# Order of the first blocks: a quarter of a projection and x's first transposes moved, exponentials in front of a unit's passes

## The chip, the cores and the metric

The kernel runs on one core of a Trainium2 chip. Its engines are TensorE (PE; its weight loads are shown apart as PEld), VectorE (DVE), ScalarE (ACT), GpSimd (POOL) and SyncE (SP), which here only issues transfers. Every engine works through its own list of instructions in the order in which they were written; semaphores hold an instruction until what it needs is there. The metric is the device time of one execution in microseconds (us), the median of several.

## The reference

Six sub-layers of a decoder work on x, 8 sequences of 128 rows of 512 numbers, all in float32. Only the first is touched by the change; the second and the fifth matter because their preparations lie in the same stretch.

```python
x = layernorm(x + L0_attn(x))            # 8 heads of width 8, softmax over 128 keys
x = layernorm(x + L0_xattn(ctx, ctx, x)) # softmax(ctx x^T / sqrt(128)) over the keys
x = layernorm(x + L0_ffn(x))             # a routed low-rank addition
x = layernorm(x + L1_attn(x))            # weights looked up from 16-level codes
x = layernorm(x + L1_xattn(x, ctx))      # scores through Wq^T Wk
x = layernorm(x + L1_ffn(x))

def L0_attn(x):
    qk = (x @ Wqk.T + bqk).reshape(b, n, 8, 8, 2)
    v = (x @ Wv.T + bv).reshape(b, n, 8, 8)
    attn = softmax(q @ k^T) / 8
    return (attn @ v) @ Wo.T + bo
```

L1_attn's weights are `NF4[codes] * scales`: an integer code of 0 to 15 picks one of 16 numbers, and a scale per 64 columns multiplies it.

## The kernel before

The 1024 rows of x are cut into 8 tiles of 128, one to a sequence. The first attention is a loop over these tiles, called blocks here, t = 0 to 7. PE's part of block t is, in order: `max_rows(t)` (turns the row maxima of the scores), `o_proj(t-1)` (the output projection of the tile before), `scores_T(t)` (the scores again, transposed and with the maximum subtracted), `x_T(0, t-2)` (the normed x of two tiles before, transposed for the second sub-layer), `scores(t+1)`, and `heads_out(t)` (probabilities times values). Between them stand pieces of work that belong to later sub-layers and fill PE's time: `key_step(n)`, n = 0 to 15, four products each of which sum up to one quarter of Wq^T Wk in PSUM bank 0, and `key_biases`. In blocks 3, 4 and 5 four key steps run: one behind `max_rows`, one behind `scores_T`, and two behind `heads_out`. The first of these last two starts a new quarter in bank 0 and so waits on `kw_ready`, until ACT has copied the quarter before out of the bank. In block 6 `key_biases(4)` waits in the same way at the end.

ACT's part of block t from t = 2 on is `unit_bends(t-1, 0)`, `heads_exp(t)` (the exponentials of `scores_T(t)`), `x_T_out(t-2)` (copies the transposes to SBUF), `key_group_out` (the copy of a finished quarter that `kw_ready` stands for), `unit_bends(t-1, 1)` and `norm_tail(t-1)` (the last step of the layer norm). A bend is one pass over 128x1024 codes with a piecewise linear function; six passes and two joins on DVE look up one chunk of L1_attn's weights. `unit_bends(u, part)` is one or two passes: for odd u one pass in each part, for even u two. So part 0 of block t has one pass at t = 2, 4, 6 and two at t = 3, 5, 7.

`scores(t+1)` waits until `heads_exp(t)` has read the scores' banks; `max_rows` waits for DVE's row maximum of the new scores; `x_T(0, t-2)` waits for `norm_tail(t-2)`. ACT's passes over the second chunk of codes wait for its transfer. DVE's share is the row maximum, the addition of the maximum to the queries, the division by the sums, the layer norm's statistics and the joins.

The order is written out by hand. Behind the loop come `sims(0)`, `o_proj(7)`, `x_T(0, 6)`, which waits for `norm_tail(6)`, and `keys(0)`, the first of the long products of the second sub-layer's stage.

Of the kernel before, what the change touches and what calls it, by code (L numbers as in the profile page):

```python
# [18 lines left out]
NT = 8  # L19
T = NT * P  # L20
D = 512
KD = D // P
# [87 lines left out]
def key_span(t):  # L110

    first = 2 + KD * (t - 3)
    return (max(0, first), min(first + KD, KD * KD))
# [22 lines left out]
def decoder_kernel(nc, i, out):  # L136
# [4 lines left out]
    with ctx:  # L141
# [3 lines left out]
        def sem(name):  # L145
            return ctx.enter_context(nc.semaphore(name))
# [252 lines left out]
        qk_ps, qk_ready, place_ps, q_placed, k_placed, v_ps, vT_ready, vt_ps, v_ready = (sem(n) for n in ("qk_ps", "qk_ready", "place_ps", "q_placed", "k_placed", "v_ps", "vT_ready", "vt_ps", "v_ready"))  # L399
# [202 lines left out]
        def _(pe):  # L602
# [10 lines left out]
                for n in range(times):  # L613
                    pe.matmul(bank[1][:, 0:HG * P], mz[:, 0, :], mz_flat, start=True, stop=True)

            def qk_projection(n):

                if n == 0:
                    pe.wait_ge(in_qk, 16)
                pe.wait_ge(in_x[n], 16)  # L620
                if n >= 2:
                    pe.wait_ge(qk_ready, (0, 0, 1, 3)[n])
                for h in range(2) if n == 0 else (0,):
                    size = P if n == 0 else PC
                    if h:
                        pe.wait_ge(in_x0b, 16)
                    t = slice(n * PC + h * P, n * PC + h * P + size)
                    for k in range(KD):
                        last = pe.matmul(bank[QK_BANK[n]][:, h * P:h * P + size], qkT[:, k, :], xT[:, k, t], start=(k == 0), stop=(k == KD - 1))
                last.then_inc(qk_ps, 1)  # L630

            def values(m):

# [12 lines left out]
            def v_rows(m):  # L646

                pe.wait_ge(vT_ready, m + 1)
                if m:
                    pe.wait_ge(ln_sum, m)  # L650
                for b in range(4):
                    h = b // 2
                    part = slice(h * HA, (h + 1) * HA)
                    dst = bank[V_BANK[h]][:, PC + b % 2 * HA:PC + (b % 2 + 1) * HA]
                    last = pe.transpose(dst, vT[part, m * PC + b % 2 * P:m * PC + (b % 2 + 1) * P], ident[part, part])
                last.then_inc(vt_ps, 1)
# [10 lines left out]
            def scores(b):  # L667
                if b >= 2:
                    pe.wait_ge(in_heads[b // 2], 16 * HI)
                else:  # L670
                    pe.wait_ge(q_placed, 1)
                    pe.wait_ge(k_placed, 1)
                if b >= 1:
                    pe.wait_ge(p_ready, b)
                t = slice(b * P, (b + 1) * P)
                for g in range(HG):
                    for n in range(HI):
                        rows = slice(n * ROWG, n * ROWG + HK)
                        last = pe.matmul(head_scores[:, n, g, :], qT[rows, g, t], kT[rows, g, t], start=True, stop=True)
                last.then_inc(s_ps, 1)  # L680

            def max_rows(b):

                pe.wait_ge(max_ready, b + 1)
                for g in range(HG):
                    last = pe.transpose(max_T[:, g, :], mz[:, g, :], ident[:, :])
                last.then_inc(max_ps, 1)

            def scores_T(b):
                pe.wait_ge(aug_ready, b + 1)  # L690
                t = slice(b * P, (b + 1) * P)
                for g in range(HG):
                    for n in range(HI):
                        rows = slice(n * ROWG, n * ROWG + HK)
                        last = pe.matmul(head_scores[:, n, g, :], kT[rows, g, t], q_aug[rows, b % 2, g, :], start=True, stop=True)
                last.then_inc(sT_ps, 1)

            def heads_out(b):

                pe.wait_ge(p_ready, b + 1)  # L700
                pe.wait_ge(v_ready, b // 4 + 1)
                if b >= 1:
                    pe.wait_ge(att_ready, b)
                for cols, lhs in ((slice(0, P), lambda g, n: vx[:, b, g, n, :]), (slice(P, 2 * P), lambda g, n: ones8[:, g, :])):
                    for g in range(HG):
                        for n in range(HI):
                            last = pe.matmul(bank[1][n * ROWG:(n + 1) * ROWG, cols], lhs(g, n), pT[:, b % 2, n, g, :],
                                             start=(g == 0), stop=(g == HG - 1))
                last.then_inc(pv_ps, 1)

            def o_proj(b):
                pe.wait_ge(att_ready, b + 1)
                if b == 0:
                    pe.wait_ge(in_xn, 48)
                else:
                    pe.wait_ge(ln_sum, b)
                    pe.wait_ge(v_ready, 2)
                pe.matmul(bank[7][:, :], attT[:, b % 2, :], wo0[:, :], start=True, stop=True).then_inc(o_ps, 1)
# [13 lines left out]
            def key_step(n):  # L732

                c, d = divmod(n, KD)
                if n == 0:
                    pe.wait_ge(qk_ready, NP)
                    pe.wait_ge(in_wk, 16 * KD)
                    pe.wait_ge(in_wq, 16)
                elif d == 0:
                    pe.wait_ge(kw_ready, c)  # L740
                last = pe.matmul(bank[0][:, :], wk1[d][:, c * P:(c + 1) * P], wq1[:, d, :], start=(d == 0), stop=(d == KD - 1))  # L741
                if d == KD - 1:
                    last.then_inc(kw_ps, 1)
# [68 lines left out]

            warm_up(WARM)
            qk_projection(0)
            warm_up(2)
            place_heads()
# [2 lines left out]
            values(0)  # L819
            pe.wait_ge(ident_ready, 1)  # L820
            max_rows(0)
            v_rows(0)
            scores_T(0)
            qk_projection(2)
            scores(1)
            heads_out(0)
            values(1)
            for t in range(1, NT):
                steps = range(*key_span(t)) if t > 1 else range(0)
                max_rows(t)  # L830
                for n in steps[0:1] if 2 < t < NT - 1 else ():
                    key_step(n)
                if t == 2:
                    v_rows(1)
                    key_step(0)
                o_proj(t - 1)
                scores_T(t)
                if t == 1:
                    qk_projection(3)
                elif t == NT - 1:  # L840
                    key_biases(KD + 1)
                for n in steps[1:2]:
                    key_step(n)
                if t > 1:
                    x_T(0, t - 2)
                if t + 1 < NT:
                    scores(t + 1)
                heads_out(t)
                for n in steps[2:]:
                    key_step(n)  # L850
                if t == NT - 2:
                    key_biases(KD)
# [329 lines left out]
            def t_products(j, b):  # L1182

                w = t_dn_part(j)
                return down_products(t_d_bank(b)[:, :], b, (hidden_part(xh, j), hidden_part(xl, j)), (w, w), j == 0, j == T_END[-1])
# [23 lines left out]
            for b in range(NT):  # L1209
                for j in T_END:  # L1210
                    if b == 0:
                        t_landed(j)
                    last = t_products(j, b)
# [4 lines left out]
        def _(act):  # L1218
# [43 lines left out]
            def unit_bends(u, part):  # L1262

                early_bends(2 * u + part + LEAD)
# [19 lines left out]
            def key_group_out(c):  # L1284
                act.wait_ge(kw_ps, c + 1)
                if c < KD:
                    nc.scalar.activation(kq_w[:, c, :], bank[0][:, :], ACT.Copy).then_inc(kw_ready, 1)
                else:
                    nc.scalar.activation(folded[:, c - KD, :], bank[0][:, :], ACT.Copy).then_inc(kw_ready, 1)
# [26 lines left out]
            def heads_exp(b):  # L1316
                act.wait_ge(sT_ps, b + 1)
                if b >= 2:
                    act.wait_ge(pv_ps, b - 1)
                nc.scalar.activation(pT[:, b % 2, :, :, :].rearrange("p i g t -> p i (g t)"),  # L1320
                                     head_scores.rearrange("p i g t -> p i (g t)"), ACT.Exp).then_inc(p_ready, 1)
# [26 lines left out]
            for t in range(2, NT):  # L1348
                if t == NT - 1:
                    key_group_out(KD)  # L1350
                unit_bends(t - 1, 0)
                heads_exp(t)
                x_T_out(t - 2)
                if t > 2:
                    key_group_out(t - 3 if t < NT - 1 else KD + 1)
                unit_bends(t - 1, 1)
                norm_tail(t - 1)
# [976 lines left out]
```

## Time and profile before

| | us |
|---|---|
| median of 3 runs | 644.88 (644.25 to 645.72) |
| the profiled execution's own time | 645.23 |
| its span in the trace | 643.1 |
| PE busy | 632.0 |
| DVE busy | 396.3 |
| ACT busy | 381.6 |

The granted clock of PE over the execution was 0.998 of full speed. The blocks 1 to 7 lie between 21 and 70 us of the span, `x_T(0, 6)` at 72.6. Busy time is the time in which an engine has an instruction under way. A start and a duration are given for each group of instructions; consecutive instructions of one engine overlap by some 0.1 us, so that what one costs its engine in a row is the distance from its start to the next start. PE is busy for nearly all of the span; the time in brackets behind a row is how long its engine had been idle.

### The profile page before, as it was taken

Reading aid. Unit: us, or ns where it says so; the run is one execution under the profiler, and the core shown is the slowest. Engines: PE = TensorE matmul, PEld = TensorE weight load, DVE = VectorE, ACT = ScalarE, POOL = GpSimd, SP = SyncE. Lnnn points to the kernel's source line nnn. Section 1 sums busy time; section 2 is a strip of 40 time slices with the busy share of each in tenths; the row PEclk is TensorE's granted clock in tenths of the full one; section 3 lists DMA queues with packets and bytes.
Section 4 is the critical chain, followed back from the end, with each engine's and each line's share of the span. In section 5 each row is a group of like instructions: output and inputs, shape, how many; then the busy total and the mean of one; then the engine's idle time right before and its main releaser. Section 6 shows DMA issues by size and latency. Waiting matters only on the chain.

```text
span 643.1 us, 8521 instructions
## 1 busy us (share of the span) xinstructions
PE 632.0 (98%) x3226; PEld 470.0 (73%) x3226; DVE 396.3 (62%) x633; ACT 381.6 (59%) x527; POOL 65.0 (10%) x116
## 2 busy tenths in 40 slices
PE   9999999999999999999999999999999999999996
PEld 6655555544558888888888888887777888888874
DVE  4798787667988777767667355335655212125467
ACT  2977789976987697576675154223565343316532
POOL 1032142311330000000000000001211000000012
PEclk9999999999999999999999999999999999999999
DMA  7771585512253134233320003056010322100002
GB/s 246 288 243 52 188 268 172 162 52 92 81 152 120 39 110 139 73 104 111 94 83 2 1 1 131 1 216 274 1 33 2 115 77 88 33 1 0 1 33 99
DMA packets 25590, 63.92 MB, mean 99 GB/s; under 512 B 5541, under 2 KB 10725, under 8 KB 24782
## 3 DMA queue, kind: packets, MB, share of 16 engines
q1 hardware_dynamic: 23294, 61.68, 29.4%
q10 hardware_dynamic: 2256, 1.70, 0.8%
q8 instruction: 26, 0.43, 0.3%
q14 instruction: 14, 0.11, 0.1%
HBM read 58.77 MB, written 4.60 MB: 99 GB/s over the span
## 4 chain that ended last, share of the span: by engine, by line
PE 88%; DVE 4%; ACT 4%; DMA 1%; issue 1%; SPq 1%; POOL 0%; POOLq 0%; DVEq 0%; ACTq 0%
PE bank L1043 18%; PE bank L1031 8%; PE bank L1030 8%; PE bank L1032 8%; PE bank L1122 8%; PE bank L1121 8%; PE bank L882 4%; PE bank L802 3%; PE bank L606 3%; PE bank L741 2%; PE bank L1097 1%; DMA codes<-in_c_qkv 1%; PE bank L912 1%; PE bank L926 1%; PE bank L984 1%
## 5 line engine op out<-in xcount | busy, mean ns | idle before, releaser
L1232 ACT ACTIVATE line<-line 128x1024 f32<-128x1024 f32 x87 | 91.4, 1050 | 0.2
L1030 PE MATMUL bank<-xh,wh 128*128 128x512 f32 x224 | 87.5, 391 | 0.0
L1031 PE MATMUL bank<-xl,wh 128*128 128x512 f32 x224 | 87.5, 391 | 0.0
L1032 PE MATMUL bank<-xh,wl 128*128 128x512 f32 x224 | 87.3, 390 | 0.0
L1043 PE MATMUL bank<-wh,xh 128*128 128x512 f32 x192 | 76.1, 396 | 0.2 <-DVE xl L2128 0.2
L1043 PE MATMUL bank<-wh,xl 128*128 128x512 f32 x192 | 74.9, 390 | 0.0
L2211 DVE SCALAR_TENSOR_TENSOR arena<-bank,ff_s,arena 128x512 f32<-128x512 f32 x28 | 21.0, 752 | 72.9 <-PE bank L1122 63.8
L2128 DVE TENSOR_TENSOR xl<-arena,xh 128x1024 fp32r<-128x1024 f32 (+1 forms) x26 | 29.7, 1141 | 35.4 <-ACT xh L1536 35.3
L1121 PE MATMUL bank<-xh,wh 128*128 128x512 f32 x128 | 50.3, 393 | 0.0
L1536 ACT ACTIVATE xh<-arena 128x1024 fp32r<-128x1024 f32 (+1 forms) x26 | 25.6, 991 | 41.3 <-PE bank L1043 34.8
L1122 PE MATMUL bank<-xl,wh 128*128 128x512 f32 x128 | 49.9, 390 | 0.0
L1032 PEld LDWEIGHTS bank<-xh,wl 128*128 128x128 f32 x224 | 42.1, 188 | 8.8
L1030 PEld LDWEIGHTS bank<-xh,wh 128*128 128x128 f32 x224 | 42.1, 188 | 8.5
L1031 PEld LDWEIGHTS bank<-xl,wh 128*128 128x128 f32 x224 | 42.1, 188 | 8.5
L1630 ACT ACTIVATE arena<-bank,ff_s 128x512 f32<-128x512 f32 x28 | 19.2, 686 | 43.4 <-PE bank L1122 43.4
L1512 ACT ACTIVATE arena<-bank 128x512 f32<-128x512 f32 x28 | 16.4, 586 | 46.9 <-PE bank L1032 46.9
L1695 POOL TENSOR_TENSOR rstd<-rstd,minus_half 128x1 f32<-128x1 f32 x40 | 26.7, 668 | 172.1 <-DVE rstd L2149 162.4
L1043 PEld LDWEIGHTS bank<-wh,xh 128*128 128x128 f32 x192 | 36.1, 188 | 8.3 <-DVE xl L2128 0.6
L1043 PEld LDWEIGHTS bank<-wh,xl 128*128 128x128 f32 x192 | 36.1, 188 | 7.5
L1121 PE MATMUL bank<-xh,wl 128*128 128x512 f32 x96 | 37.6, 391 | 0.0
L1745 DVE SCALAR_TENSOR_TENSOR line<-line 128x1024 f32<-128x1024 f32 x29 | 35.3, 1218 | 3.6 <-ACT line L1232 3.2
L1043 PE MATMUL bank<-wl,xh 128*128 128x512 f32 x96 | 37.4, 390 | 0.0
(219 smaller groups left out, 1264.3 us busy)
## 6 DMA issues: line engine op xcount, KB each, us to landing
codes<-in_c_gu SPq DMA_DIRECT2D x14, 512.0 KB, 3.8
scales<-in_s_gu SPq DMA_DIRECT2D x28, 256.0 KB, 4.0
codes<-in_t_gu SPq DMA_DIRECT2D x8, 512.0 KB, 4.2
codes<-in_c_dn SPq DMA_DIRECT2D x7, 512.0 KB, 4.6
scales<-in_s_dn SPq DMA_DIRECT2D x14, 256.0 KB, 3.9
fold<-in_t_dn SPq DMA_DIRECT2D x1, 3584.0 KB, 15.7
codes<-in_c_qkv SPq DMA_DIRECT2D x6, 512.0 KB, 4.8
scales<-in_t_gu SPq DMA_DIRECT2D x6, 512.0 KB, 3.8
```

The source lines that it names most:

```text
L882: pe.matmul(bank[FF_BANK[b % 3]][:, :], xT[:, k, b * P:(b + 1) * P], w0T[:, k, :], start=(k == 0), stop=False)
L1030: pe.matmul(dst, wh[:, s, c:c + P], xh[:, k, cols], start=(k == 0), stop=False)
L1031: pe.matmul(dst, wh[:, s, c:c + P], xl[:, k, cols], start=False, stop=False)
L1032: last = pe.matmul(dst, wl[:, s, c:c + P], xh[:, k, cols], start=False, stop=(k == KD - 1))
L1043: ins = pe.matmul(dst, h[:, b * P:(b + 1) * P], w, start=first and p == 0, stop=last and p == len(hiddens) - 1)
L1121: pe.matmul(dst, w[:, c:c + P], xh[:, k, cols], start=(k == 0), stop=False)
L1122: last = pe.matmul(dst, w[:, c:c + P], xl[:, k, cols], start=False, stop=(k == KD - 1))
L1232: nc.scalar.activation(below(slot), below(slot), ACT.Prelu, bias=bias, scale=scale, alpha=alpha).then_inc(bent, 1)
L1536: nc.scalar.activation(dst[:, cols], hT[:, j, cols], ACT.Copy).then_inc(done, 1)
L1695: last = nc.gpsimd.tensor_tensor(rstd[:, m % 2, 1:2], rstd[:, m % 2, 0:1], minus_half[:, :], ALU.pow)
L1745: nc.vector.scalar_tensor_tensor(weight(slot), weight(slot), -NEAR_UP, below(slot), ALU.max, ALU.subtract).then_inc(joined, 1)
L2128: nc.vector.tensor_tensor(low[:, cols], hT[:, j, cols], f32(hi[:, cols]), ALU.subtract).then_inc(done, 1)
```

## The change

Three things move; nothing is added or taken away.

- A quarter of a projection. `qk_projection(2)` is a sum over four parts of the 512 columns, each one product of 128x128 by 128x256. Its first part is now issued behind `max_rows(0)` and in front of `v_rows(0)`; the other three stay behind `scores_T(0)`. Both pieces add into bank 0.
- x's first transposes. `x_T(0, 0)` in block 2 stood in front of `scores(3)` and now stands behind `heads_out(2)`. The lines on `key_step` are written in another way, with the same order.
- Exponentials. In the blocks 2 to 7 ACT now does `heads_exp(t)` first and `unit_bends(t-1, 0)` behind it.

```diff
-            def qk_projection(n):
+            def qk_projection(n, steps=range(KD)):
...
-                    for k in range(KD):
+                    for k in steps:
                         last = pe.matmul(bank[QK_BANK[n]][:, h * P:h * P + size], qkT[:, k, :], xT[:, k, t], start=(k == 0), stop=(k == KD - 1))
-                last.then_inc(qk_ps, 1)
+                if KD - 1 in steps:
+                    last.then_inc(qk_ps, 1)
...
             max_rows(0)
+            qk_projection(2, range(1))
             v_rows(0)
             scores_T(0)
-            qk_projection(2)
+            qk_projection(2, range(1, KD))
...
                 max_rows(t)
-                for n in steps[0:1] if 2 < t < NT - 1 else ():
-                    key_step(n)
                 if t == 2:
                     v_rows(1)
-                    key_step(0)
+                for n in steps[0:1] if t < NT - 1 else ():
+                    key_step(n)
                 o_proj(t - 1)
...
-                if t > 1:
+                if t > 2:
                     x_T(0, t - 2)
                 if t + 1 < NT:
                     scores(t + 1)
                 heads_out(t)
+                if t == 2:
+                    x_T(0, 0)
                 for n in steps[2:]:
                     key_step(n)
...
             for t in range(2, NT):
                 if t == NT - 1:
                     key_group_out(KD)
+                heads_exp(t)
                 unit_bends(t - 1, 0)
-                heads_exp(t)
                 x_T_out(t - 2)
```

PE's list in block 2 before, from `scores_T(2)` on: L695 is `scores_T`, L741 a key step, L606 `x_T`, L679 `scores`, L707 `heads_out`, L686 `max_rows`.

```order
50 L695 MATMUL bank<-fold,heads 128x128 [waits aug_ready]
51 L695 MATMUL bank<-fold,heads 128x128 x7
52 L741 MATMUL bank<-arena 128x512
53 L606 MATMUL bank<-ident,x 128x128 [waits v_ready,ln_done]
54 L606 MATMUL bank<-ident,x 128x128 x3
55 L679 MATMUL bank<-heads 128x128 [waits p_ready,in_heads1]
56 L679 MATMUL bank<-heads 128x128 x7
57 L707 MATMUL bank<-fold,project 32x128 [waits att_ready,v_ready,p_ready]
58 L707 MATMUL bank<-fold,project 32x128 x7
59 L707 MATMUL bank<-fold 32x128 x8
```

The same place in the changed kernel, where every line number above 625 is one higher:

```order
53 L742 MATMUL bank<-arena 128x512
54 L680 MATMUL bank<-heads 128x128 [waits p_ready,in_heads1]
55 L680 MATMUL bank<-heads 128x128 x7
56 L708 MATMUL bank<-fold,project 32x128 [waits att_ready,v_ready,p_ready]
57 L708 MATMUL bank<-fold,project 32x128 x7
58 L708 MATMUL bank<-fold 32x128 x8
59 L606 MATMUL bank<-ident,x 128x128 [waits v_ready,ln_done]
60 L606 MATMUL bank<-ident,x 128x128 x3
61 L687 MATMUL bank<-ident,fold 128x128 [waits max_ready]
```

The four transposes have moved from in front of the scores to between `heads_out(2)` and `max_rows(3)`.

ACT's list in block 3 before: L1224, L1226, L1232 and L1240 are passes over codes, L1320 the exponentials, L1274 `x_T_out`, L1287 `key_group_out`, L1281 `norm_tail`.

```order
31 L1224 ACTIVATE line<-codes 128x1024 [waits joined,in_codes0]
32 L1226 ACTIVATE line<-codes 128x1024
33 L1320 ACTIVATE fold<-bank 128x1024 [waits pv_ps,sT_ps]
34 L1274 ACTIVATE arena<-bank 128x4x128 [waits xt_ps]
35 L1287 ACTIVATE fold<-bank 128x512 [waits kw_ps]
36 L1232 ACTIVATE line<-line 128x1024 [waits bent]
```

And in the changed kernel, where these numbers are three higher:

```order
31 L1323 ACTIVATE fold<-bank 128x1024 [waits pv_ps,sT_ps]
32 L1227 ACTIVATE line<-codes 128x1024 [waits joined,in_codes0]
33 L1229 ACTIVATE line<-codes 128x1024
34 L1277 ACTIVATE arena<-bank 128x4x128 [waits xt_ps]
35 L1290 ACTIVATE fold<-bank 128x512 [waits kw_ps]
36 L1235 ACTIVATE line<-line 128x1024 [waits bent]
```

The two passes now stand between the exponentials and the two copies out of PSUM. Blocks 5 and 7 read alike; in blocks 2, 4 and 6 it is one pass.

## Rows read from the trace of the kernel before

**Rows 1.** The page: busy us, share of the span, instructions.

```profile
PE 632.0 (98%) x3226; PEld 470.0 (73%) x3226; DVE 396.3 (62%) x633; ACT 381.6 (59%) x527; POOL 65.0 (10%) x116
```

**Rows 2.** The chain of waits in order of time: start us, us, what.

```profile
19.06 7.09 DMA codes<-in_c_qkv
...
71.84 0.71 ACT x L1281
```

**Rows 3.** Timeline of PE, block 0: start us, us, instructions [idle before, released by].

```profile
15.05 0.34 PE L655 MATMUL bank<-ident,project 64*128 64x64 f32 x4 [0.27 <-ACT project L1308]
15.32 0.73 PE L695 MATMUL bank<-fold,heads 9*128 9x128 f32 x16
15.98 1.99 PE L629 MATMUL bank<-arena,early_w 128*128 128x256 f32 x8
17.91 0.73 PE L679 MATMUL bank<-heads 9*128 9x128 f32 x16
```

**Rows 4.** Timeline of PE, blocks 2 and 3.

```profile
30.17 0.73 PE L695 MATMUL bank<-fold,heads 9*128 9x128 f32 x16
30.82 1.13 PE L741 MATMUL bank<-arena 128*128 128x512 f32 x2
31.79 0.60 PE L606 MATMUL bank<-ident,x 128*128 128x128 f32 x4
32.77 0.73 PE L679 MATMUL bank<-heads 9*128 9x128 f32 x16 [0.38 <-ACT fold L1320]
...
34.84 0.44 PE L686 MATMUL bank<-ident,fold 128*128 128x128 f32 x2 [0.33 <-DVE fold L1852]
...
40.89 1.98 PE L741 MATMUL bank<-arena 128*128 128x512 f32 x4
```

**Rows 5.** Timeline of ACT, blocks 2 and 3.

```profile
30.68 1.04 ACT L1232 ACTIVATE line<-line 128x1024 f32<-128x1024 f32 x1
31.62 1.00 ACT L1320 ACTIVATE fold<-bank 128x1024 f32<-128x1024 f32 x1
...
37.87 1.02 ACT L1320 ACTIVATE fold<-bank 128x1024 f32<-128x1024 f32 x1 [0.90 <-PE bank L695]
39.33 0.60 ACT L1274 ACTIVATE arena<-bank 128x512 f32<-128x512 f32 x1 [0.44 <-PE bank L606]
39.83 0.59 ACT L1287 ACTIVATE fold<-bank 128x512 f32<-128x512 f32 x1
```

**Rows 6.** Timeline of PE, blocks 4 to 6: `key_step(8)`, `key_step(12)`, `key_biases(4)`.

```profile
48.56 1.98 PE L741 MATMUL bank<-arena 128*128 128x512 f32 x4
...
56.23 1.98 PE L741 MATMUL bank<-arena 128*128 128x512 f32 x4
...
63.78 1.04 PE L752 MATMUL bank<-arena,k_b 128*1 128x512 f32 x8
```

**Rows 7.** Timeline of ACT, exponentials of blocks 4 to 7 and `x_T_out(5)`.

```profile
45.54 1.02 ACT L1320 ACTIVATE fold<-bank 128x1024 f32<-128x1024 f32 x1 [1.59 <-PE bank L695]
...
53.21 1.02 ACT L1320 ACTIVATE fold<-bank 128x1024 f32<-128x1024 f32 x1 [1.58 <-PE bank L695]
...
60.88 1.02 ACT L1320 ACTIVATE fold<-bank 128x1024 f32<-128x1024 f32 x1 [1.59 <-PE bank L695]
...
67.34 1.02 ACT L1320 ACTIVATE fold<-bank 128x1024 f32<-128x1024 f32 x1
68.87 0.60 ACT L1274 ACTIVATE arena<-bank 128x512 f32<-128x512 f32 x1 [0.50 <-PE bank L606]
```

**Rows 8.** Timeline of PE: `o_proj(7)`, `x_T(0, 6)`; of ACT: `key_columns_out`.

```profile
71.32 1.12 PE L718 MATMUL bank<-arena,fold 128*128 128x512 f32 x2 [0.39 <-DVE fold L1868]
...
72.60 0.66 PE L606 MATMUL bank<-ident,x 128*128 128x128 f32 x4
...
77.82 0.18 ACT L1293 ACTIVATE wb<-bank 128x8 f32<-128x8 f32 x1 [2.15 <-PE bank L763]
```

**Rows 9.** Windows at the end: window, us, busy us of each engine, PEclk, DMA.

```profile
638.00:643.10 5.10, 0.00 (x0) 0.00 (x0) 2.18 (x6) 0.67 (x1) 0.55 (x1) 0.74 0.29 103
```

## The prediction, as it was put on record before the run

> **What bounds the kernel now.** I read the page's busy times first: PE is busy for 632.0 of 643.1 us [rows 1], so a change of order can win only PE's few gaps, and loses whatever new gap it makes. Next I read PE's timeline through the blocks for the gaps. The change can reach three: 0.27 in front of `v_rows(0)` at 15.05 [rows 3], 0.38 in front of `scores(3)` at 32.77 and 0.33 in front of `max_rows(3)` at 34.84 [rows 4]. The chain of waits says what ends the second: the transfer of the second chunk of codes, 19.06 to 26.15, then ACT's passes without a pause, then the exponentials of block 2, then `scores(3)` [rows 2, 5]; the third gap is released by DVE's row maximum of these scores [rows 4]. ACT's timeline comes last. In blocks 3 to 6 ACT stands idle 0.90, 1.59, 1.58 and 1.59 us in front of its exponentials, released by `scores_T` [rows 5, 7]. The passes that the change moves run today ahead of that wait, so they are free; and since those exponentials start when PE delivers, putting them first in the list does not make them earlier. Only block 2's are held by the pass itself (30.68, then 31.62, back to back [rows 5]).
>
> **The quarter of the projection.** It moves 2 of 8 records (a product is two records here). They cost a quarter of the distance from 15.98 to 17.91, 0.48 us [rows 3]. `max_rows(0)` is issued by 14.78 (15.05 less the 0.27), so `v_rows(0)` starts at 15.26 and `scores_T(0)` 0.27 later at 15.53, 0.21 later than now. The rest of the projection is 1.45, and `scores(1)` starts at 15.53 + 0.66 + 1.45 = 17.64 and not 17.91: PE is 0.27 ahead. No row shows a sum that is interrupted in its bank; from the nearest rows I bound what that costs between nothing and one more wait like the one removed, 0.27, and take nothing. The 0.27 does not reach the end by itself, since the exponentials of block 2 hang from the transfer at 26.15, which the move does not touch; but it lets `scores_T(2)` end at 30.17 + 0.73 - 0.27 = 30.63 [rows 4], just in time for exponentials that can then start at 30.68. Without it they would start at 30.95.
>
> **Block 2, exponentials and transposes.** The exponentials start at 30.68 and not 31.62, 0.94 earlier [rows 5], and `scores(3)` with them: 32.77 - 0.94 = 31.83. PE gets there with `key_step(1)` at 30.82 - 0.27 + 0.97 = 31.52 [rows 4], so a wait of 0.3 remains even with the transposes gone from there. Behind `scores(3)` now: `max_rows(3)` follows its start by 34.84 - 32.77 = 2.07 (DVE's maximum), so not before 33.90; PE fills that with `scores` 0.65, `heads_out` 1.02 and the four transposes 0.5, in all 2.17, and so starts `max_rows(3)` at about 34.03. That is **0.81 ahead** of 34.84, and the whole gain: `o_proj(2)`, `scores_T(3)` and the exponentials of block 3 come 0.81 earlier, at 37.87 - 0.81 = 37.06. For the transposes' new place the nearest rows give 0.44 to 0.60 for four; I take 0.5.
>
> **Blocks 3 and 5, two passes each.** Here the moved passes lie in front of something PE waits for. Before, from the start of the exponentials in block 3: 1.02, a wait of 0.44 for the transposes, `x_T_out` at 39.33, the copy of the quarter at 39.83, ended 40.42; `key_step(4)` started at 40.89 without an idle mark [rows 4, 5]. There were 0.47 us of slack. Now: exponentials 0.92 to the next start (1.02 less the overlap of 0.1), two passes of 0.95 each (30.68 to 31.62 is one [rows 5]), `x_T_out` 0.49, the copy's 0.59 and 0.05 to PE: 0.92 + 1.90 + 0.49 + 0.59 + 0.05 = 3.95. So `key_step(4)` can't start before 37.06 + 3.95 = 41.01, while PE is ready at 40.89 - 0.81 = 40.08. **PE loses 0.93** in front of `key_step(4)` and is 0.12 behind from there. In block 5 the exponentials start at 53.21 + 0.12 = 53.33 and `key_step(12)` not before 57.28; PE is ready at 56.35 [rows 6, 7]. **0.93 more**, so 1.05 behind. Nothing else is there for PE to do: the key step waits at the head of its list, and behind it `max_rows`, whose input DVE has long made.
>
> **Blocks 4 and 6, one pass each.** The sum is 0.95 shorter, 3.00. Block 4: 45.54 + 0.12 + 3.00 = 48.66 against PE ready at 48.56 + 0.12 = 48.68, nothing. Block 6: 60.88 + 1.05 + 3.00 = 64.93 against 63.78 + 1.05 = 64.83 [rows 6, 7], 0.10, so 1.15 behind.
>
> **Block 7.** The exponentials start at 67.34 as soon as the passes in front of them and `scores_T(7)` are through together, and `x_T(0, 6)` at 72.60 waits for `norm_tail(6)`, 71.84 to 72.55 on the chain [rows 2, 7, 8]. From the exponentials' start to `x_T(0, 6)` it is 5.26 now, with 0.50 of waiting for transposes in it. With two passes between: 0.92 + 1.90 + 0.49 + 0.48 + two further passes 1.90 + `norm_tail` 0.81 (0.71 and the overlap of 0.1) + 0.06 = 6.56. ACT idles instead in front of the exponentials, where it wins nothing, since `scores_T(7)` comes with PE. **1.30 more.**
>
> **The sum.** -0.81 + 0.93 + 0.93 + 0.10 + 1.30 = 2.45 behind at `x_T(0, 6)`. Behind it PE goes into `keys(0)` and is dense; ACT waits 2.15 for PE at 77.82 [rows 8] and so starts level with PE again, and later waits hang from PE's own work. I carry the 2.45 to the end in full: 645.23 + 2.45 = 647.7 for an execution like the profiled one, whose own time lies 0.35 above the median; on the median 644.88 + 2.45 = **647.3 us**.
>
> **Ends of the range.** The slack in front of the copies (0.47) and each pass are known to some 0.05, times five blocks 0.3 both ways. If the interrupted sum costs 0.27 the exponentials of block 2 start at 30.95 and the gain is 0.54: +0.27. DVE's joins read what the passes make. The join of chunk 2 has several us, the second join of chunk 3 in block 7 about 1; if such a join came late, DVE would stall up to one pass, 0.95, in front of the addition for the attention: 648.3. At the other end stands the absorption below, 646.0.
>
> **Rivals.** (a) *The loss of block 7 is swallowed.* `norm_tail(6)` late by 1.30 would cost nothing if something behind it took the slack: +1.15, 646.0. For it: ACT's wait of 2.15 at 77.82. Against: this is slack of ACT and not of PE, and `keys(0)` stands behind `x_T(0, 6)` in PE's list. (b) *Not slower: only the waits of block 2 decide.* If the copies were still in time for the key steps, the 0.81 of block 2 would be all that is left: 644.1. The point from which it decides is the time that the moved passes take: it holds as long as they fit into the wait for transposes and the slack, 0.44 + 0.47 = 0.91 [rows 4, 5]. One pass (0.95) nearly does, two (1.90) don't. For it: the order on ACT puts first what PE asks for first. It would take passes at half their time. (c) *The clock falls in the new gap.* In front of `x_T(0, 6)` PE would stand idle some 1.5 us (0.16 now, from 71.32 + 1.12 to 72.60, and 1.30 [rows 8]). In the last 5.10 us of the span, where PE has no work, the granted clock is 0.74 on average, so part of them at 1.2 GHz [rows 9]. If the stretch behind the gap ran at that level, 3.4 us of key products would take 3.4 more: 650.7. Against: the gap of 0.39 at 71.32 [rows 8] left the mean of the whole execution at 0.998, and 1.5 is nearer to 0.39 than to 5.10. The Trainium skill states the mechanism (TensorE: Matmul & The Clock Gate, "Part 1: The HAM clock gate"): the half rate is the array's default, and only activity lifts it. The windows at the end agree, with 0.74 once PE has nothing left; no row here shows a gap between 0.4 and 5 us. (d) *The order does not reach the chip as written*: no, the lists of both engines show it.
>
> **Chances.** A measurement of this kernel tells 0.2%, 1.3 us, from no change. The forecast (both stalls of 0.93 and the 1.30 reach the end) 0.76; a join or another wait late on top, up to 648.3, 0.05; (c) 0.03; all three are slower: 0.84. (a) 0.08 and the larger part of (b) (0.05 of 0.08) lie within 0.2%: 0.13; the rest, 0.03, would be (b) with the 0.39 in front of `o_proj(7)` gone too, 1.2 and at the bound, faster. The range of eight in ten goes from 645.9, just under (a), to 648.3.
>
> **What would show it.** Right: PE idle of some 0.9 us in front of `key_step(4)` and `key_step(12)`, released by ACT's L1290; of some 1.5 in front of `x_T(0, 6)`, released by `norm_tail`; the gap in front of `v_rows(0)` gone, a wait of 0.3 in front of `scores(3)`, `max_rows(3)` at 34.0; ACT's wait for `scores_T` longer by the passes and its wait in front of `x_T_out` gone in blocks 3 to 7. Wrong: key steps 4 and 12 without idle time in front of them, or the difference at `x_T(0, 6)` larger than that at the end of the span. A time under 646.2 would say that the stalls are not there or are taken back.

## The result, and the profile after

| | before | after |
|---|---|---|
| median, us | 645.22 (5 runs) | 647.72 (647.32 to 648.29, 5 runs) |
| span of the profiled execution | 643.1 | 645.7 |
| PE busy | 632.0 | 631.5 |
| PE's start of `x_T(0, 6)` | 72.60 | 75.24 |

The ratio is 1.0038, 95% interval 1.0027 to 1.0049: 2.50 us slower, where 2.45 had been worked out. The predicted time, 647.3, was built on a median of 644.88; with two more runs of the kernel before that median is 645.22, and the measured 647.72 is 2.50 above it. Three single executions far outside all others (1065.95 us in `no_proj`, 1949.10 in `codes_first`, 1637.55 in the kernel before) were in a slow state and stand in no figure below. PE is busy for as long as before (631.5 and 632.0 us); the time is in its gaps. PE reaches `x_T(0, 6)` 2.64 later than before and the span ends 2.6 later, so nothing is taken back behind it. What PE waited for in the first 90 us of the changed kernel, in total, times, longest:

```profile
PE bank L742 <- ACT fold L1290: 1.7, 2, 0.8
PE bank L606 <- ACT x L1284: 1.4, 1, 1.4
...
PE bank L680 <- ACT fold L1323: 0.8, 1, 0.8
```

L1290 is the copy of a quarter (`key_group_out`), L742 a key step; L1284 is `norm_tail`, L606 the transposes. Neither of the first two waits is among the gaps of the kernel before [rows 4, 6]. PE's timeline in the changed kernel, block by block (start us, us, group, idle before and its releaser):

```profile
14.46 0.60 PE L629 MATMUL bank<-arena,early_w 128*128 128x256 f32 x2
14.99 0.34 PE L656 MATMUL bank<-ident,project 64*128 64x64 f32 x4
15.27 0.73 PE L696 MATMUL bank<-fold,heads 9*128 9x128 f32 x16
15.92 1.56 PE L629 MATMUL bank<-arena,early_w 128*128 128x256 f32 x6
17.41 0.73 PE L680 MATMUL bank<-heads 9*128 9x128 f32 x16
...
32.30 0.73 PE L680 MATMUL bank<-heads 9*128 9x128 f32 x16 [0.84 <-ACT fold L1323]
...
33.97 0.66 PE L606 MATMUL bank<-ident,x 128*128 128x128 f32 x4
34.46 0.38 PE L687 MATMUL bank<-ident,fold 128*128 128x128 f32 x2
...
41.35 1.98 PE L742 MATMUL bank<-arena 128*128 128x512 f32 x4 [0.85 <-ACT fold L1290]
...
49.02 1.98 PE L742 MATMUL bank<-arena 128*128 128x512 f32 x4
...
57.60 1.98 PE L742 MATMUL bank<-arena 128*128 128x512 f32 x4 [0.85 <-ACT fold L1290]
...
65.24 1.04 PE L753 MATMUL bank<-arena,k_b 128*1 128x512 f32 x8
...
72.69 1.12 PE L719 MATMUL bank<-arena,fold 128*128 128x512 f32 x2 [0.39 <-DVE fold L1871]
75.24 0.66 PE L606 MATMUL bank<-ident,x 128*128 128x128 f32 x4 [1.43 <-ACT x L1284]
```

The moved quarter fills the gap of [rows 3]: `v_rows(0)` at 14.99 has no idle mark. The split sum costs next to nothing: its two pieces take 0.53 (14.46 to 14.99) and 1.49 (15.92 to 17.41), 2.02 together, for 1.93 in one piece [rows 3]. The gap in front of `max_rows(3)` [rows 4] is gone too, filled by the transposes at 33.97. Then come the new ones: 0.85 in front of `key_step(4)` at 41.35 and `key_step(12)` at 57.60, 1.43 in front of `x_T(0, 6)`. ACT's timeline shows from the other side why:

```profile
26.64 1.06 ACT L1227 ACTIVATE line<-codes 128x1024 f32<-128x1024 int32 x1 [1.29 <-DMA codes<-in_c_qkv]
...
31.15 1.00 ACT L1323 ACTIVATE fold<-bank 128x1024 f32<-128x1024 f32 x1
...
34.66 0.60 ACT L1277 ACTIVATE arena<-bank 128x512 f32<-128x512 f32 x1 [1.56 <-PE bank L606]
...
37.41 1.02 ACT L1323 ACTIVATE fold<-bank 128x1024 f32<-128x1024 f32 x1 [0.50 <-PE bank L696]
38.33 1.05 ACT L1227 ACTIVATE line<-codes 128x1024 f32<-128x1024 int32 x1
39.27 1.05 ACT L1229 ACTIVATE line<-codes 128x1024 f32<-128x1024 int32 x1
40.22 0.59 ACT L1277 ACTIVATE arena<-bank 128x512 f32<-128x512 f32 x1
40.70 0.60 ACT L1290 ACTIVATE fold<-bank 128x512 f32<-128x512 f32 x1
...
53.66 1.02 ACT L1323 ACTIVATE fold<-bank 128x1024 f32<-128x1024 f32 x1 [3.08 <-PE bank L696]
```

From the exponentials at 37.41 to `key_step(4)` at 41.35 it is 3.94, with both passes inside. In front of the exponentials of block 5 ACT now idles 3.08 where it idled 1.58 [rows 7]: the passes stood in a wait of ACT, where they were free, and now stand on PE's path.

### The profile page after: what moved, and what is told of

It is laid out like the page before. It is cut to its first block, busy times and chain, and to the rows that moved or that the text cites. A ratio compares the mean times of both kernels' runs of the same rounds, so it can differ in the third digit from the quotient of the medians.

```text
span 645.7 us, 8522 instructions
## 1 busy us (share of the span) xinstructions
PE 631.5 (98%) x3226; PEld 469.2 (73%) x3226; DVE 396.3 (61%) x633; ACT 381.1 (59%) x527; POOL 65.0 (10%) x116
## 4 chain that ended last, share of the span: by engine, by line
PE 86%; ACT 5%; DVE 4%; DMA 2%; issue 2%; SPq 1%; POOL 0%; POOLq 0%; DVEq 0%; ACTq 0%
PE bank L1046 18%; PE bank L1034 8%; PE bank L1033 8%; PE bank L1035 8%; PE bank L1125 8%; PE bank L1124 8%; PE bank L885 4%; PE bank L803 3%; PE bank L606 3%; PE bank L742 2%; PE bank L1100 1%; DMA codes<-in_c_qkv 1%; PE bank L915 1%; PE bank L929 1%; PE bank L987 1%
## 5 line engine op out<-in xcount | busy, mean ns | idle before, releaser
L1125 PE MATMUL bank<-xl,wl 128*128 128x512 f32 x96 | 37.4, 389 | 0.0
```

What stands on the lines that cost most here:

```text
L1125: last = pe.matmul(dst, w[:, c:c + P], xl[:, k, cols], start=False, stop=(k == KD - 1))
```

## The experiments

Every kernel is timed against the kernel before on the same chip; the figure ahead is the difference of the medians in us, and the ratio has its 95% interval. An interval of 0.0009 on either side of a ratio is about 0.6 us.

**The exponentials alone, `exp_only`.** Edit on the kernel before:

```diff
+                heads_exp(t)
                 unit_bends(t - 1, 0)
-                heads_exp(t)
```

> Only the exponentials are put in front of the passes, in blocks 2 to 7; the projection and the transposes stay where they were. Theory (the passes stand in front of copies that PE waits for): stalls of 0.93 in front of key_step(4) and key_step(12), 0.10 in front of key_biases(4), 1.30 more in front of x_T(0, 6), less a gain in block 2 that is 0.46 to 0.54 and not 0.81, since scores_T(2) now ends last: +2.75, some 0.3 above the changed kernel's +2.5. Rival (the later transposes hold ACT, and the order of the exponentials costs nothing): -0.5 to 0.

Measured: +2.68, ratio 1.0042 (1.0028 to 1.0056). PE waits 0.85, 0.85 and 1.43 at the same three places as in the changed kernel. The order on ACT by itself is enough for all of the loss.

**Blocks apart: `exp_35`, `exp_46`, `exp_7`.** The kernel before with the exponentials first in some blocks alone:

```diff
+                if t in (3, 5):        # (4, 6), (7,)
+                    heads_exp(t)
                 unit_bends(t - 1, 0)
-                heads_exp(t)
+                if t not in (3, 5):
+                    heads_exp(t)
```

> The kernel before with the exponentials first in blocks 3 and 5 alone (two passes each). Theory: two stalls of 0.93 in front of key_step(4) and key_step(12), +1.9, both carried to the end. Rival (the waits of the blocks behind absorb it, so that only the last stall counts): +0.9 or less.

> The same in blocks 4 and 6 alone (one pass each). Theory: one pass, 0.95, fits into the wait for the transposes and the slack, 0.91 to 0.95: 0.0 to +0.1. Rival (every pass behind the exponentials costs PE its length or half of it): +1 to +1.9.

> The same in block 7 alone (two passes). Theory: norm_tail(6) is late by 1.30, x_T(0, 6) with it, and PE carries it to the end: +1.3. Rival (ACT's slack of 2.15 behind it takes it): 0 to +0.3.

Measured: blocks 3 and 5 +1.66, ratio 1.0028 (1.0017 to 1.0039); blocks 4 and 6 -0.16, 0.9998 (0.9989 to 1.0007); block 7 +1.31, 1.0026 (1.0014 to 1.0038). PE's waits for ACT, in `exp_35`:

```profile
41.75 1.98 PE L741 MATMUL bank<-arena 128*128 128x512 f32 x4 [0.85 <-ACT fold L1287]
...
58.00 1.98 PE L741 MATMUL bank<-arena 128*128 128x512 f32 x4 [0.85 <-ACT fold L1287]
```

and in `exp_7`:

```profile
73.61 0.66 PE L606 MATMUL bank<-ident,x 128*128 128x128 f32 x4 [1.43 <-ACT x L1281]
```

Two stalls of 0.85 are 1.70, and the runs lose 1.66: each reaches the end whole. One pass is hidden, two are not. Block 7's loss reaches the end as well, so rival (a) of the prediction is out: ACT's slack behind `norm_tail(6)` is no slack of PE.

**Copies ahead of the passes, `copies_first`.** Edit on the changed kernel:

```diff
                 heads_exp(t)
-                unit_bends(t - 1, 0)
+                if t in (2, NT - 1):
+                    unit_bends(t - 1, 0)
                 x_T_out(t - 2)
                 if t > 2:
                     key_group_out(t - 3 if t < NT - 1 else KD + 1)
+                if t not in (2, NT - 1):
+                    unit_bends(t - 1, 0)
```

> The changed kernel, but in blocks 3 to 6 the passes stand behind both copies (exponentials, x_T_out, key_group_out, passes); block 7 as in the changed kernel. Theory: what costs is the passes between the exponentials and the copies, so the stalls at key_step(4), key_step(12) and key_biases(4) are gone, 1.96 of the 2.45, and block 7 stays: +0.5 against the kernel before. Rival (ACT is simply short of time in these blocks, wherever the passes stand): +2.0 to +2.5.

Measured: +0.64, ratio 1.0012 (1.0003 to 1.0020), against +2.50 for the changed kernel. The exponentials stand in front of the passes in both; only the copies have changed places with the passes. ACT is not short of time in these blocks. What cost was the passes between the exponentials and a copy for which PE waits. The trace of this run has no wait left in front of `key_step(4)` and `key_step(12)`, and the 1.43 in front of `x_T(0, 6)` still there.

**The quarter of the projection: `proj_only` and `no_proj`.** The first is the kernel before with the quarter moved, the second the changed kernel without that move:

```diff
             max_rows(0)
+            qk_projection(2, range(1))
             v_rows(0)
             scores_T(0)
-            qk_projection(2)
+            qk_projection(2, range(1, KD))
```

> Only the quarter of the projection is moved. Theory: PE is 0.3 to 0.4 ahead from scores(1) on, and gives all of it back in front of scores(3), whose wait grows from 0.38 to 0.7, because that hangs from the codes' transfer by way of ACT: 0.0 (within 0.2). Rival (PE's lead reaches the end): -0.3 to -0.4. Second rival (an interrupted sum costs something): +0.3.

> The changed kernel without the move of the projection's quarter: x_T(0, 0) moved and the exponentials first. Theory: scores_T(2) ends 0.27 to 0.37 later and holds the exponentials of block 2 back, so the gain there is 0.5 and not 0.81: +2.75. Rival (the quarter's move costs time, as its own run leaves possible with +0.46 in an interval from -0.1 to +1.0): below +2.4.

Measured: moved alone +0.46, ratio 1.0007 (0.9999 to 1.0016); the changed kernel without it +2.60, 1.0038 (1.0025 to 1.0052). In `proj_only` the lead is handed back in front of `scores(3)`, as expected, though the wait grew to 0.99 and not to 0.7:

```profile
33.39 0.73 PE L680 MATMUL bank<-heads 9*128 9x128 f32 x16 [0.99 <-ACT fold L1322]
```

PE is 0.33 ahead behind the move (from `max_rows(0)` to `max_rows(1)` it is 6.77 and not 7.10), and the other 0.27 or so of the longer wait is the codes, which landed later in this execution. By time the move is worth nothing that can be told from zero: its own run leans to a small loss, `no_proj` against the changed kernel (+2.60 against +2.50) to a small gain, neither clear. The intervals are too wide to rule out the 0.27 of the prediction; the traces say more. In `no_proj` the exponentials of block 2 start at 30.80, 0.98 behind the start of the pass ahead of them, where the changed kernel has 0.94 (30.21 to 31.15): they are held by 0.04 and not by 0.27. PE and the transfer that ACT's passes hang from do not stand at the same distance in every execution: in `exp_only`, where ACT's passes found their codes without a wait, the same exponentials waited 0.63 for `scores_T(2)`.

**Block 2's exponentials: `exp2_proj` and `exp2_only`.** The kernel before with the exponentials first at t = 2 alone (`if t in (2,)` in the edit above), with and without the quarter.

> The exponentials are first in block 2 alone, and the projection's quarter is moved; the transposes stay. Theory: the gain of block 2 is kept whole and none of the later stalls is made: -0.83, with scores(3) starting right behind the transposes and max_rows(3) still waiting some 0.4 for DVE. Rival (block 2's gain is given back at the next waits on ACT): 0.

> The exponentials first in block 2 alone, nothing else moved. Theory: block 2's gain with scores_T(2) ending last: -0.46 to -0.54, some 0.3 less than with the projection's quarter moved as well (expected -0.83, measured -0.58). Rival (the quarter's move costs time): -0.8 to -1.0.

Measured: -0.58, ratio 0.9989 (0.9980 to 0.9997), and -0.62, 0.9990 (0.9982 to 0.9999). These two are some 0.1% ahead of the kernel before and 0.5% ahead of the changed one. The gain is kept to the end, and the exponentials alone are enough for it: the 0.3 that the quarter was expected to add does not show in the times (0.04 the other way, well inside the intervals), and in the trace of `exp2_only` the exponentials are held by 0.08 (1.02 from pass to exponentials, and not 0.94). In `exp2_proj` PE has no wait left in front of `scores(3)`; the one in front of `max_rows(3)` stays, as expected:

```profile
34.55 0.44 PE L687 MATMUL bank<-ident,fold 128*128 128x128 f32 x2 [0.33 <-DVE fold L1857]
```

**The transfer, `codes_first`.** Edit on the kernel before, on SP's queue:

```diff
+            sp.dma_start(codes[:, 1, :], i["c_qkv"][1]).then_inc(in_codes[1], 16)
             for d in range(KD):
                 sp.dma_start(wk1[d], i["wk1"][d]).then_inc(in_wk, 16)
-            sp.dma_start(codes[:, 1, :], i["c_qkv"][1]).then_inc(in_codes[1], 16)
```

> The kernel before, with the transfer of the second chunk of codes issued ahead of the four of wk1 on SP's queue. Theory (scores(3) hangs from that transfer by way of ACT's passes): the codes are there some 2 us earlier, ACT's passes start by 25.8 without a wait, the wait of 0.38 in front of scores(3) is gone or nearly so: -0.3 to -0.4, unless wk1 comes too late for key_step(0) at 28, which would show as a wait there. Rival (the place on the queue does not matter, since the transfers share the engines): 0.

Measured: -0.51, ratio 0.9991 (0.9982 to 1.0000). ACT's timeline has the passes without a wait ahead, and the exponentials 5.4 behind their start, as before:

```profile
25.18 1.05 ACT L1224 ACTIVATE line<-codes 128x1024 f32<-128x1024 int32 x1
...
30.62 1.00 ACT L1320 ACTIVATE fold<-bank 128x1024 f32<-128x1024 f32 x1
```

PE's wait in front of `scores(3)` is gone and `key_step(0)` has none. The direction is right; the size, at the edge of its interval, is no more than likely.

**The transposes alone, `xt_only`.** Edit on the kernel before:

```diff
-                if t > 1:
+                if t > 2:
                     x_T(0, t - 2)
...
                 heads_out(t)
+                if t == 2:
+                    x_T(0, 0)
```

> Only x_T(0, 0) is moved behind heads_out(2). Theory: with the exponentials behind the passes, scores(3) still starts when block 2's exponentials end, so nothing is won there but the gap in front of max_rows(3); x_T_out(0) waits for the later transposes with all of ACT behind it, some 1.7 us, of which block 3's wait in front of its exponentials (0.90) takes a part: exponentials of block 3 late by some 1.1 after four passes in a row, a wait of about 1.1 in front of scores(4), +1.05 at the end. Rival (the transposes only fill a gap): -0.3.

Measured: +2.75, ratio 1.0042 (1.0029 to 1.0054): the theory's +1.05 and the rival's -0.3 are both missed. The waits are those of the theory, 1.07 in front of `scores(3)` and 0.89 in front of `scores(4)`:

```profile
33.15 0.73 PE L679 MATMUL bank<-heads 9*128 9x128 f32 x16 [1.07 <-ACT fold L1322]
33.81 1.08 PE L707 MATMUL bank<-fold,project 128*32 128x128 f32 x16
34.66 1.08 PE L707 MATMUL bank<-fold 128*32 128x128 f32 x16
35.68 1.12 PE L606 MATMUL bank<-ident,x 128*128 128x128 f32 x4
...
42.02 0.73 PE L679 MATMUL bank<-heads 9*128 9x128 f32 x16 [0.89 <-ACT fold L1322]
```

But `heads_out` takes 1.08 for each half and the transposes 1.12, where the changed kernel has 0.64, 0.62 and 0.66 for the same work at 32.96 to 34.6. Windows of the same execution (window, us, PE, PEld, DVE, ACT, POOL busy, PEclk, DMA):

```profile
31.00:33.00 2.00, 1.08 (x6) 0.26 (x2) 1.93 (x4) 2.00 (x3) 0.77 (x1) 1.00 0.37 74
33.00:34.00 1.00, 0.85 (x20) 0.76 (x24) 0.32 (x2) 0.01 (x1) 0.92 (x2) 0.89 0.83 164
34.00:35.00 1.00, 1.00 (x24) 0.92 (x22) 1.00 (x1) 0.00 (x0) 0.27 (x1) 0.50 0.94 372
...
36.00:37.00 1.00, 1.00 (x6) 1.00 (x5) 0.97 (x2) 0.17 (x1) 0.00 (x0) 0.50 0.09 20
37.00:38.00 1.00, 1.00 (x5) 0.52 (x4) 0.84 (x3) 1.00 (x2) 0.00 (x0) 0.91 0.34 91
```

The granted clock is 0.50, the lower level of 1.2 GHz, from shortly before 34 to shortly after 37. The other four executions of this kernel, not profiled, took 647.28 to 648.44 and had a mean clock of 0.994 to 0.997, so the loss is in every one of them.

**The gap filled, `xt_filled`.** `xt_only` with two products that nothing reads, in front of `scores(3)` of block 2:

```diff
                 if t > 2:
                     x_T(0, t - 2)
+                if t == 2:
+                    for n in range(2):
+                        pe.matmul(bank[1][:, 0:HG * P], mz[:, 0, :], mz_flat, start=True, stop=True)
```

> The kernel with only x_T(0, 0) moved, and two products without use (128x128 by 128x256, into bank 1, which nothing holds there) in PE's gap in front of scores(3); they take 0.9 of its 1.07 us. Theory (that kernel's excess over the +1.05 of its waits, 1.7, is PE at 1.2 GHz from 34 to 37 us, after the gap): the granted clock stays 1.00 through block 2, and the time falls by 1.5 to 1.7 to +1.0 to +1.3 over the kernel before, although PE does more. Rival (the excess is waiting for ACT and DVE): no change, +2.7 to +2.9.

Measured: +1.37, ratio 1.0020 (1.0011 to 1.0029), 1.4 less than `xt_only` with more work on PE, and a little short of the 1.5 to 1.7 expected. All 11 executions (646.07 to 647.06) lie under the lowest of `xt_only`. Its timeline and its window:

```profile
31.85 1.03 PE L848 MATMUL bank<-fold 128*128 128x256 f32 x4
33.05 0.73 PE L679 MATMUL bank<-heads 9*128 9x128 f32 x16 [0.17 <-ACT fold L1325]
33.70 0.64 PE L707 MATMUL bank<-fold,project 128*32 128x128 f32 x16
...
34.71 0.66 PE L606 MATMUL bank<-ident,x 128*128 128x128 f32 x4
...
40.60 0.73 PE L679 MATMUL bank<-heads 9*128 9x128 f32 x16 [1.02 <-ACT fold L1325]
```

```profile
34.00:37.00 3.00, 3.00 (x41) 1.72 (x30) 2.97 (x5) 1.59 (x3) 0.27 (x1) 1.00 0.41 137
```

The clock stays at 1.00, the durations are the full level's, and the wait of 1.02 in front of `scores(4)` is still there. So the transposes' move alone costs about 1.4 by waiting, and the other 1.4 was the clock.

## Why the prediction was right

The sum as predicted, as the profiled pair has it (differences of PE's starts against [rows 4, 6, 8]), and as the runs priced it alone:

| step | predicted | profiled pair | alone |
|---|---|---|---|
| block 2, at `max_rows(3)` | -0.81 | -0.38 | -0.58 and -0.62 |
| `key_step(4)` | +0.93 | +0.84 | with the next |
| `key_step(12)` | +0.93 | +0.91 | +1.66 for both |
| blocks 4 and 6 | +0.10 | 0.00 | -0.16 |
| block 7 | +1.30 | +1.27 | +1.31 |
| sum | +2.45 | +2.64 | +2.2 |

The mechanism was right: the order on ACT alone makes the whole loss, the stalls stand where they were put, and taking the passes from between exponentials and copies removes two of the three. That the sum came within 0.05 us is luck in part. The gain of block 2 was worked out too large by 0.2 (runs alone) to 0.4 (profiled pair), and the losses, 3.26 in all, by 0.5 and 0.2; these errors cancel, and each interval is about 0.6 us on either side. One slip changes nothing: 31.83 + 2.17 is 34.00 and not 34.03, so that the prediction's own terms give -0.84 for block 2.

**The losses** were right in place, mechanism and size. The rule that decided them, passes free while they fit into 0.44 + 0.47, holds in the runs: one pass costs nothing, and two cost 0.84 and 0.91 by PE's starts (0.85 each time by its idle marks) where 0.93 had been worked out. The 0.10 of block 6 is there in front of `key_biases(4)` (+1.46 against +1.37 ahead of it) and is taken back at `o_proj(6)`, whose wait shrinks from 0.30 to 0.22. The prediction left that wait out.

**The gain of block 2** was too large in the profiled pair for a reason that the prediction named as the anchor of the chain but did not put into the range. The chain of waits of the changed kernel has the transfer as

```profile
19.61 7.02 DMA codes<-in_c_qkv
```

The codes landed at 26.63 and not at 26.15 [rows 2], and ACT's passes, the exponentials at 31.15 and `scores(3)` at 32.30 all came 0.47 later than worked out. PE, by its lead of 0.33, was there before, so that the wait in front of `scores(3)` was 0.84 and not the 0.3 of the prediction. The landing moves from one execution to the next, and not visibly with the change: ACT's first pass on these codes starts 11.82 behind `max_rows(0)` in the trace of the kernel before and 12.45 in the changed kernel's, but 12.0 to 12.1 in eight of the other twelve traces, with the quarter moved or not. A sum anchored in one execution's landing carries that spread. Measured against its own landing the block went as predicted: the exponentials start 4.51 behind the first pass (26.64 to 31.15), 0.94 less than before. The experiment on the transfer agrees that this is what `scores(3)` hangs from.

**The quarter of the projection** was overrated in the traces, and its worth is not settled by the times. The lead came out nearly as worked out, 0.33 for 0.27, with the sum in two pieces. But the prediction turned all of the lead into a gain by way of `scores_T(2)`, and the traces without the quarter have that hold at 0.04 and 0.08. The rest of the lead is handed back as idle time in front of `scores(3)`, 17 us later.

**Rivals.** (a) is ruled out by `exp_7`. (b) is out, since two passes do not fit; the gain that it would have left stands in `exp2_only` and `exp2_proj`, with the order of block 2 alone. (c) did not happen in the profiled execution of the changed kernel, and its five timed executions have mean clocks of 0.997 to 0.999. The granted clock around the longest new gap of the changed kernel, and behind it:

```profile
73.70:75.30 1.60, 0.17 (x2) 0.06 (x2) 1.44 (x3) 1.60 (x3) 0.00 (x0) 1.00 0.00 0
75.30:78.00 2.70, 2.70 (x14) 1.74 (x14) 2.60 (x8) 1.74 (x4) 0.55 (x1) 1.00 0.81 279
```

It may have happened once in `exp_7`, which has the same gap of 1.43: one of its 11 executions took 650.05 us, 3.5 over their median, with a mean clock of 0.992 against 0.998 or 0.999 in the others. That is the size that (c) named, 3.4, but the execution was not profiled, so where its clock fell is not shown. A fall is shown in `xt_only`, behind a shorter gap.

**The transposes.** The change's parts are not additive: the transposes' move, which costs 2.75 alone, costs nothing that can be told beside the exponentials (+2.60 with both and no quarter, +2.68 with the exponentials alone). In the changed kernel ACT waits 1.56 for the late transposes and 0.50 for `scores_T(3)`; in `exp_only` it waits 2.36 for `scores_T(3)` at once. So the first wait falls where ACT would have waited in any case. The prediction counted it as nothing without saying so.

## What to carry to other kernels

An instruction that stands ahead of a wait on its own engine is free up to the length of that wait; moved behind it, it is paid for by whoever waits next on that engine, as far as it is longer than the room there. So before putting "the urgent one first", read what ended the wait in front of it: if the other engine delivers it only then, being first wins nothing, and only a block in which the pass itself ended last (here block 2 of six) is worth the change. Check every copy out of PSUM behind the new place against its slack, pass by pass: here 0.91 us of room held one pass and not two.

## What the runs showed of the hardware that was not expected

PE's granted clock fell to 0.50 for 3.4 us (33.8 to 37.2) behind a gap of 1.07 us in `xt_only`, and at 1.2 GHz `heads_out` took 1.08 a half for 0.64. In the profiled executions it did not fall behind 1.43 us in the changed kernel and `exp_7`, 0.99 in `proj_only` or 1.02 in `xt_filled`. The Trainium skill (TensorE: Matmul & The Clock Gate, "Part 1: The HAM clock gate") calls half rate the default, which activity lifts; the return to 1.00 at 37.2, with PE busy without a break, agrees with it.

What told these gaps apart is open, and the nearest rows do not tell it either. In `xt_only` PE was busy for 1.08 of the 2.00 us from 31.00, then ran the scores, products of 9 rows, and fell. In `proj_only` the two us in front of the same scores read:

```profile
31.40:33.40 2.00, 1.01 (x7) 0.52 (x6) 1.71 (x3) 2.00 (x3) 1.21 (x2) 1.00 0.36 90
```

PE did even less there, the scores follow in the same way, and the clock stays at 1.00 to the end of the blocks. That filling the gap kept the clock is shown; that neither the length of the gap nor the busy share in front of it decides by itself is shown too.
